# A decoder layer on one core, with the written order of its steps replaced on all five queues

## What is computed

```python
x = x + attn(layernorm(x))                 # 8 heads of 128, one shared k and v, causal
x = x + cross_attn(layernorm(x), ctx, bias, mask)
                                           # 16 heads of 16; bias is 32 x 16 x 256 x 256, added twice
x = x + moe(layernorm(x))                  # 8 experts of 256 hidden, top 2 by a gate, and a shared one
```

## Time and profile before

| | us |
|---|---|
| runs of the kernel before (3) | 2540.53, 2551.84, 2554.71 |
| median | 2551.84 |
| the profiled execution, its own time | 2536.33 |
| its span, first to last instruction | 2534.5 |
| busy: PE, ACT, DVE, POOL | 2153.5, 2085.8, 1929.3, 1785.0 |
| TensorE's mean granted clock | 0.937 of full |

### The profile page before, as it was taken

How to read it: one execution, slowest core, us unless ns; L and a number is a source line. 1 busy time by engine, 2 the same in 40 slices (tenths; PEclk the granted TensorE clock), 3 DMA queues, 4 the chain that set the end, 5 groups by cost and what they waited for, 6 DMA issues and landing times.

```text
span 2534.5 us, 73035 instructions
## 1 busy us (share of the span) xinstructions
PE 2153.5 (85%) x24128; PEld 1861.8 (73%) x24128; DVE 1929.3 (76%) x6672; ACT 2085.8 (82%) x6065; POOL 1785.0 (70%) x1899
## 2 busy tenths in 40 slices
...
GB/s 151 131 142 149 157 143 135 164 137 151 162 141 135 162 147 145 162 154 132 152 161 137 153 159 143 141 157 143 151 157 149 132 155 148 155 147 158 138 124 34
DMA packets 711785, 367.16 MB, mean 145 GB/s; under 512 B 561393, under 2 KB 659953, under 8 KB 711409
## 3 DMA queue, kind: packets, MB, share of 16 engines
...
## 4 chain that ended last, share of the span: by engine, by line
PE 51%; issue 14%; ACT 11%; DVE 10%; DMA 9%; POOL 3%; SPq 1%; DVEq 0%; ACTq 0%; POOLq 0%
PE ps_a_misc L966 10%; PE ps_c_out L966 10%; PE ps_c_hidden L966 10%; DMA b_probsT_hi_lo<-b_probs_hi_lo 8%; PE ps_a_scores L1026 4%; PE ps_b_misc L1103 3%; PE ps_b_scores L1089 3%; PE ps_a_misc L1045 2%; DVE b_probs_hi_lo L836 2%; ACT ps_b_probs L665 2%; PE ps_c_hidden L993 2%; ACT ps_b_probs L663 2%; DVE g_mask L899 2%; ACT b_probs_hi_lo L673 2%; PE ps_b_misc L966 1%
## 5 line engine op out<-in xcount | busy, mean ns | idle before, releaser
L521 POOL TENSOR_TENSOR bias<-bias,b_mask 128x512 f32<-128x512 f32 x512 | 640.8, 1274 | 93.7 <-DVE b_mask L815 88.5
L829 DVE CUSTOM_DVE_ANT_0 b_neg_scores<-ps_b_scores,bias 128x256 f32<-128x256 f32 x1024 | 390.5, 418 | 168.7 <-PE ps_b_scores L1089 158.3
L836 DVE TENSOR_TENSOR b_probs_hi_lo<-ps_b_probs,b_probs_hi_lo 128x512 f16<-128x512 f32 x512 | 351.0, 686 | 103.2 <-ACT b_probs_hi_lo L673 101.5
L535 POOL TENSOR_TENSOR c_hidden<-c_relu 128x512 f32<-128x512 f32 x288 | 299.9, 1041 | 180.4 <-ACT c_relu L691 156.9
L542 POOL TENSOR_TENSOR c_hidden_lo<-c_hidden,c_hidden_hi 128x512 f16<-128x512 f32 x288 | 333.8, 1159 | 118.2 <-issue 67.9
L966 PE MATMUL ps_c_out<-w_hi,c_hidden_hi 128*128 128x256 f16 x1152 | 320.7, 278 | 99.9 <-DVE acc L929 67.6
L663 ACT ACTIVATE ps_b_probs<-b_neg_scores,b_neg_max 128x256 f32<-128x256 f32 x512 | 246.6, 482 | 171.1 <-DVE b_probs_hi_lo L836 110.9
L966 PE MATMUL ps_c_hidden<-c_xT_hi,w_hi 128*128 128x256 f16 x1152 | 319.9, 278 | 3.9 <-DVE c_xT_lo L744 2.4
L966 PE MATMUL ps_c_out<-w_hi,c_hidden_lo 128*128 128x256 f16 x1152 | 321.4, 279 | 0.0
L966 PE MATMUL ps_c_out<-w_lo,c_hidden_hi 128*128 128x256 f16 x1152 | 321.2, 279 | 0.0
L966 PE MATMUL ps_c_hidden<-c_xT_lo,w_hi 128*128 128x256 f16 x1152 | 319.1, 277 | 0.0
...
## 6 DMA issues: line engine op xcount, KB each, us to landing
bias<-in_bias SPq DMA_DIRECT2D x256, 512.0 KB, 4.3
q_stack<-qk_scratch SPq DMA_DIRECT2D x256, 64.0 KB, 5.3
...
k_stack_even<-qk_scratch SPq DMA_DIRECT2D x128, 64.0 KB, 5.3
```

The costliest lines, as they stand in the source:

```text
L521: gp.tensor_tensor(part, part, b_mask[:, :], ALU.add).then_inc(b_c_ok, 1)
L535: gp.tensor_tensor(c_h[:, :], c_r[:, e % 2, :], c_r[:, e % 2, :], ALU.mult).then_inc(c_sq_ok, 1)
L829: last = dve.tensor_tensor_reduce(out=b_t[:, u, c, :], in0=ps_bs[:, c * T:(c + 1) * T], in1=bias[:, slot, at:at + T], scale=-2.0, scalar=3 ...
L836: dve.tensor_tensor(b_p2[:, j % DEPTH, :, 1, :], ps_bp[:, :].rearrange("p (c t) -> p c t", c=CT), b_p2[:, j % DEPTH, :, 0, :], ALU.subtrac ...
```

## The change

The five tables hold the same steps with the same arguments, in another order, and `LAGS` is 6 and no longer 5. The point of the cycle at which an iteration is cut is another one too, which by itself shifts numbers behind the `@` and changes nothing; the order is to be compared from one and the same step on. The diff, cut to the first line of each table:

```diff
     sync="""
-        b_load:1@4 b_pT:2@4 b_pT:3@4 b_load:2@4 b_pT:4@4 a_T:0@3 b_pT:5@4 b_load:3@4 a_ln:0@3 b_pT:6@4 b_pT:7@4
...
+        b_load:7@5 b_store_q:0@4 b_pT:14@5 b_mask:0@4 b_store_k:0@4 b_pT:15@5 b_stack_q:0@4 b_stack_k:0@4
...
     gpsimd="""
-        b_comb:1@4 b_comb:2@4 a_q:3@3 b_comb:3@4 b_comb:4@4 b_comb:5@4 c_ln:0@5 b_comb:6@4 b_comb:7@4 b_kv:0@3
...
+        b_v:0@4 b_comb:5@4 a_q:3@3 b_comb:6@4 c_ln:0@5 b_res:0@4 c_f1:0@5 c_lo:0@5 c_f1:1@5 c_lo:1@5 b_kv:0@3
...
     tensor="""
-        a_s:5@2 a_pt:2@2 b_wo:0@4 a_pv:1@2 a_pt:3@2 a_s:6@2 b_s:0@3 b_s:1@3 a_pv:2@2 c_T:0@4 a_pt:4@2 a_s:7@2
...
+        b_s:1@4 a_pt:3@3 c_T:0@5 b_s:2@4 a_pv:2@3 a_s:7@3 c_f1:0@5 a_pt:4@3 b_s:3@4 c_gate:0@5 c_f1:1@5 a_pv:3@3
...
-LAGS = 5
+LAGS = 6
```

76 lines of the change are left out of this document (37 added, 39 removed).

## The result

The changed kernel takes 2482.28 us (median of four runs, 2478.08 to 2486.5); beside it, on the same chip, the kernel before takes 2546.19 us (2540.0 to 2554.71). The ratio is 0.975, with a 95% interval of 0.972 to 0.979: it is faster. The profiled execution has a span of 2480.6 us and a time of its own of 2482.43.

The account below looks back on a forecast made before the run. It took waits in the window behind `b_kv:0`, set by SP's DMA backlog, as the bound: 1.47 + 1.7 - 0.3 - 0.4 = 2.47 us a period, times 29 is 72 us, giving 2465, median 2480; range 2420 to 2555.

Parts of the forecast that it names:

- SP, the bias loads, 1.7 us: Bias loads issued earlier leave the DMA backlog, shortening the window (`b_kv:0`'s end to `b_s:0`) by 1.7 us, bounds 0 to 2.36.
- SP's own chain: Next bound on the window: last probabilities, transpose issue, 16 stack loads and last landing, 14.9 to 18.0 us.
- PE, 1.47 us: `a_q:1` and `a_s:0` move behind `b_kv:0`, `a_pt:3` leaves the window: 1.47 us a period saved in the rest.
- The gate chain, 0: VectorE's `c_gate:7` goes ahead of `c_f2:0`, `b_p:4` behind `c_f2:1`: one step later, one earlier, no effect.
- `c_T`, 0.3 us lost: Around `b_s:0`, x2 and its layer norm come later behind `b_pv:15`, costing 0.3 us a period at `c_T`.
- ScalarE, 0.4 us lost: Ahead of the window ScalarE ends `b_kv` later behind PE, losing 0.4 us on the chain to `b_p:15`.
- the first: Rival: the 16 stack loads are slow by themselves, so the window does not shrink; 2529 us, chance 0.17.
- that rival: Less idle time behind `b_s:0` also keeps TensorE's clock up, 1.2 us more a period; 2445 us, chance 0.13.
- ScalarE eats the gain: Rival: ScalarE, ahead of the window, loses 2.9 us instead of 0.4, leaving no change; 2550 us, chance 0.12.
- The ring of transposes: Slower rival: with four slots, ScalarE's `b_p:10` waits for `b_pT:6`, issued later; 2602 us, chance 0.13.
- A DMA share under 1 in the window: Sign of being right: DMA engines' busy share between `b_kv:0`'s end and `b_s:0` falls under 1, from 1.08.
- The gate's wait still there: Sign of being right: PE's wait of 2.3 us at `c_f2:1` for VectorE's gate steps remains.

Follow-up runs that it names:

- old order with copies: Kernel before, each DMA transpose of `b_pT` replaced by two plain copies, so `b_pv` computes with untransposed probabilities: 2505.43 us, 0.984 of the kernel before.
- new order, copies: Changed kernel with each DMA transpose of `b_pT` replaced by two plain copies: 2467.62 us, 0.969 of the kernel before.
- old, loads early: old order with copies, only `b_load:4` to `b_load:7` moved to their places in the new SP table: 2409.52 us, 0.946 of the kernel before.
- new, loads late: new order, copies, with only `b_load:4` to `b_load:7` put back to their old SP places: 2586.84 us.
- old, `a_q:1` and `a_s:0` moved: old order with copies, both steps moved behind `b_kv:0` on PE, other engines' tables following: 2502.8 us, 0.9841 of the kernel before.
- old, GpSimd's steps late: old order with copies, GpSimd's `b_kv:0` moved behind `c_lo:1` and `b_comb:7` behind `c_lo:2`: 2582.22 us.
- new, GpSimd's steps early: new order, copies, with GpSimd's `b_kv:0` and `b_comb:7` moved ahead of its `c_f1:0`: 2376.79 us, 0.935 of the kernel before.

## Why the prediction was right, and where its steps were not

The forecast was 2480 us and the time is 2482.28. That the agreement is so close is luck. The sum said 2.47 us a period and 2465 us for the profiled execution's own time; measured were 1.39 us a period and 2482.43. The ends of the program, where 53.9 - 37 = 17 us were saved, made up for some of the difference, and the 15.5 us that I added for the median held for the kernel before only: after, the profiled execution lies at the median.

This table, means of 24 periods from the stretches, in us, is what the points below rest on. "Period" is from the stores, 27 periods. "PE work" is busy time and so depends on the clock: the mean granted clock in the window is 0.90 in the two kernels with steps late, 0.95 in the old order with copies, and 0.98 to 1.00 in the others.

| kernel | period | window | PE work in it | rest | PE work in it |
|---|---|---|---|---|---|
| before | 75.07 | 20.03 | 15.98 | 55.21 | 50.19 |
| after | 73.69 | 18.17 | 17.13 | 55.48 | 49.24 |
| old order, copies | 74.10 | 19.53 | 16.55 | 54.46 | 48.46 |
| new order, copies | 73.19 | 17.71 | 17.02 | 55.45 | 48.97 |
| old, loads early | 70.94 | 16.18 | 15.61 | 54.77 | 49.38 |
| new, loads late | 77.06 | 21.98 | 18.78 | 55.16 | 48.57 |
| old, `a_q:1` and `a_s:0` moved | 73.87 | 19.51 | 18.00 | 54.33 | 47.14 |
| old, GpSimd's steps late | 76.46 | 20.10 | 17.17 | 56.32 | 49.51 |
| new, GpSimd's steps early | 70.23 | 17.90 | 17.21 | 52.30 | 47.72 |

**SP, the bias loads, 1.7 us.** Right in kind, and the window of the changed kernel shrank by 1.86, inside the bounds. As the value of the edit it was under-sized: alone it is worth 3.2 us a period in the old order and 3.9 in the new. The upper bound of 2.36 came from PE's floor of 17.25 us, which holds only with the additional PE work; without it the window went down to 16.18. I had also placed SP's own chain next. Its parts up to the last issue add up to 4.1 + 1.23 + 7.4 = 12.7 us in the prediction, where the earlier trace rows have 15.5; the landing at the slow end of its range hid this. The chain did not get shorter, but its last part, the landing, did. And of the loads, `b_load:7` moves ahead of one transpose and not of two.

**PE, 1.47 us.** As a saving of its own this step failed. That 1.47 us of work leave the full part was right in direction (0.95 us were measured), but that the period gets shorter by it was not. The rest got 0.3 us longer, and with the edit alone the time did not change: ScalarE, which empties the bank that `b_kv:0` writes, is the next bound: PE waits for it 37.4 / 32 = 1.2 us a period. I read ScalarE's 14.53 of 15.73 us and charged 0.4 us for it on its own chain, but left the question when it would be done with `b_q`, for which PE's `b_kv:0` waits, to a rival. In the changed kernel itself, where `b_q` stands earlier on ScalarE, PE has no such wait (1.0 us in all); there other gaps of the rest grew: those of 0.50 and 0.44 us at `b_s:5` and `b_s:6`, the longer one at `c_T`, one of some 0.25 us at an `a_q`, and the gate's, which GpSimd's steps lengthen.

The two kernels with both the loads and GpSimd's steps early show it without the gate's hold-up. From the old order (70.94 us) to the new (70.23) 1.66 us of PE work leave the rest, which gets 2.47 us shorter, and 1.60 us come into the window, which gets 1.72 us longer. Once the loads are early, PE waits for only 16.18 - 15.61 = 0.57 us of the window, and work moved there lengthens it as much. So the prediction's terms of 1.47 and 1.7 us draw on one and the same wait (20.03 - 15.98 = 4.05 us before), and their sum of 3.17 is what the loads alone gave in the old order with copies (3.2).

**The gate chain, 0.** This step failed too. I compared VectorE's order, one step later and one earlier. What lengthens the chain is which instructions GpSimd runs beside it. The earlier trace rows had the clue, a wait of 2.29 us for steps of 8 elements a row. The new GpSimd table stood in the diff, with `b_kv:0` moved from ahead of `c_f1:0` to behind `c_lo:1`. I priced no step of it. It is worth 2.4 us a period in the old order and 3.0 in the new, of which (2178.8 - 2126.8) / 32 = 1.6 and 1.0 us are the clock. With GpSimd's steps early the seven gate groups take 185.0 us in the old order and 129.0 in the new: without these two steps the change would have shortened the chain.

**`c_T`, 0.3 us lost.** Its wait rose from 0.65 to 0.99 us in the mean. Right.

**ScalarE, 0.4 us lost.** Not tested by itself. The total wait of `b_s` for VectorE rose by 27 us, 0.8 us a period, which I had not forecast.

So at the level of copies -3.2 for the loads, +2.4 for GpSimd and nothing for PE's steps give -0.8, against 74.10 - 73.19 = 0.91 measured; with the prices in the new order it is -3.9 + 3.0 = -0.9. The two large terms account for the difference. What everything else that moved is worth together, two pairs show in which the loads and GpSimd's steps stand alike. With both early it is 70.94 us in the old order and 70.23 in the new (medians 2409.52 and 2376.79 us, 1.2% faster); with both late it is 76.46 and 77.06 (2582.22 and 2586.84, the same). So it is small beside the two, but not nothing: it saves 0.7 us a period once the loads and GpSimd are out of the way. That the same holds with the transposes was not tried. There the net is 1.4 us, and one reason to expect more is that `b_s:0` itself waited for the backlog.

**The rivals.** The window shrank, so the first is out. The 64 KB loads landed with a median of 3.6 in place of 5.3 us with nothing changed in them but what goes ahead. The Trainium skill, page "DMA: Bandwidth & Descriptors", section "Bandwidth", by whose rule the window would have stayed, isn't borne out here: by the prediction's estimate from that page the 16 loads would take 15.2 us whatever goes before, and from the first issue to the last landing they took 13.9 us before and 11.7 after (means of 24 periods). The clock stayed where it was on the whole (0.937 to 0.946) and is 0.70 from 1203 to 1208 us, right behind `b_s:0`, so that rival did not come true in this change; what it said of the mechanism did, once the gate's wait was gone, with about 1 us a period. "ScalarE eats the gain" was right on the place, as a bound on one term. The ring of transposes cost 0.4 us in all, in the wait of ScalarE's `b_p` for a landing:

```profile
L673 ACT ACTIVATE b_probs_hi_lo<-ps_b_probs 128x512 f16<-128x512 f32 x512 | 303.2, 592 | 4.9 <-DMA b_probsT_hi_lo<-b_probs_hi_lo 0.4
```

**The signs.** `b_pv:15` under 0.3 us: 12.4 us in all, 0.24 a period in the mean of the 24 periods, right, though 0.85 in the period shown. `b_s:0` under 1 us: 23.8 / 32 = 0.74, right. A DMA share under 1 in the window: 1.09 in the period shown, wrong there (0.97 in the mean). Stores 72 to 73 us apart: 73.69, wrong. The gate's wait still there: right, one expert on.

The best kernel found is the new order with GpSimd's two steps early, 2376.79 us with copies. Whether the changed kernel gains as much from that with its transposes was not tried, and neither was its combination with VectorE's `c_gate:8` in GpSimd's next idle time.
